# Moving two matrix products and one weight load at the start of a decoder block's turns

## The reference

```
x = x + attn(layernorm(x), ...)                       # 16 heads, stage A
x = x + gamma * xattn(layernorm(x), ctx, ctx)         # 8 heads of 64 rows, softmax over 512 columns
h1 = layernorm(x) @ w1q.T ; h3 = layernorm(x) @ w3q.T # 1365 hidden columns: "up"
x = x + (silu(h1) * h3) @ w2q.T                       # "down"
```

## Time and profile before

| | us |
|---|---|
| median of 3 runs | 1113.23 (1113.21 to 1115.01) |
| the profiled execution's own time | 1114.2 |
| its span, first to last instruction | 1112.1 |
| TensorE busy | 1104.1 |
| VectorE, ScalarE, GpSimd busy | 731.4, 550.5, 483.9 |
| DMA, mean rate | 110 GB/s |

### The profile page before, as it was taken

How to read it: one execution, slowest core, us unless ns; L and a number is a source line. 1 busy time by engine, 2 the same in 40 slices (tenths; PEclk the granted TensorE clock), 3 DMA queues, 4 the chain that set the end, 5 groups by cost and what they waited for, 6 DMA issues and landing times.

```text
span 1112.1 us, 15909 instructions
## 1 busy us (share of the span) xinstructions
PE 1104.1 (99%) x5840; PEld 938.7 (84%) x5840; DVE 731.4 (66%) x1347; ACT 550.5 (50%) x1149; POOL 483.9 (44%) x430
## 2 busy tenths in 40 slices
PE   9999999999999999999999999999999999999998
PEld 8888888878888888888888888888888888888886
DVE  7555547787777688866424334689967976887531
ACT  4556673324243376667515233167627763775130
POOL 1322327341424275665344040157728762875130
PEclk9999999999999999999999999999999999999999
DMA  7455553544533724212631112362113211310101
GB/s 246 164 189 189 185 176 129 171 126 159 173 111 93 230 96 142 86 39 86 252 114 38 38 59 65 140 205 63 53 52 101 77 49 58 113 49 1 38 1 38
DMA packets 54663, 122.20 MB, mean 110 GB/s; under 512 B 10057, under 2 KB 10057, under 8 KB 52538
## 3 DMA queue, kind: packets, MB, share of 16 engines
q1 hardware_dynamic: 54586, 121.18, 33.3%
HBM read 103.32 MB, written 17.84 MB: 109 GB/s over the span
## 4 chain that ended last, share of the span: by engine, by line
PE 94%; DVE 2%; DMA 1%; ACT 1%; issue 1%; POOL 0%; SPq 0%; POOLq 0%; DVEq 0%
PE bank L176 19%; PE bank L178 19%; PE bank L177 19%; PE bank L583 7%; PE bank L584 7%; PE bank L541 5%; PE bank L599 4%; PE bank L598 4%; PE bank L565 3%; PE bank L566 3%; PE bank L551 2%; PE bank L552 2%; DMA x1d<-x_scratch 1%; PE bank L608 0%; DVE x3l L860 0%
## 5 line engine op out<-in xcount | busy, mean ns | idle before, releaser
L583 PE MATMUL bank<-x3h,w 128*128 128x512 f32 (+2 forms) x368 | 143.5, 393 | 0.4 <-DVE x3l L860 0.3
L1471 ACT ACTIVATE yh<-bank 128x512 fp32r<-128x512 f32 x64 | 38.1, 600 | 209.9 <-PE bank L178 209.8
L584 PE MATMUL bank<-x3l,w 128*128 128x512 f32 (+2 forms) x368 | 140.6, 385 | 0.0
L940 POOL TENSOR_SCALAR pe_x<-pe_x,xri,gam 128x512 f32<-128x512 f32 x96 | 76.2, 795 | 78.5 <-DVE xri L779 76.1
L775 DVE TENSOR_REDUCE xmx<-bank 128x1 f32<-128x512 f32 x128 | 87.7, 687 | 32.9 <-PE bank L552 31.4
L2143 POOL TENSOR_TENSOR wal<-raw_a,wah 128x512 fp32r<-128x512 f32 x44 | 61.0, 1413 | 109.5 <-ACT wah L1513 109.5
L176 PE MATMUL bank<-wah,gh 128*128 128x512 f32 x256 | 102.6, 401 | 0.0
L2148 POOL TENSOR_TENSOR wbl<-raw_b,wbh 128x512 fp32r<-128x512 f32 x64 | 87.0, 1383 | 34.1 <-ACT wbh L1534 33.8
L176 PE MATMUL bank<-yh,rh 128*128 128x512 f32 x256 | 100.4, 392 | 0.8 <-DVE xacc L1979 0.8
L176 PE MATMUL bank<-wah,ph 128*128 128x512 f32 x256 | 100.1, 391 | 0.0
L177 PE MATMUL bank<-wal,gh 128*128 128x512 f32 x256 | 100.1, 391 | 0.0
(11 more groups left out here) (181 smaller groups left out, 3014.7 us busy)
## 6 DMA issues: line engine op xcount, KB each, us to landing
raw_a<-in_wk SPq DMA_DIRECT2D x8, 1024.0 KB, 5.2
raw_b<-in_wq SPq DMA_DIRECT2D x8, 1024.0 KB, 5.6
raw_a<-in_wo SPq DMA_DIRECT2D x8, 1024.0 KB, 5.1
raw_b<-in_wvt SPq DMA_DIRECT2D x8, 1024.0 KB, 5.0
ternary_scratch<-wraw SPq DMA_DIRECT2D x24, 341.2 KB, 3.0
x1d<-x_scratch SPq DMA_DIRECT2D x48, 128.0 KB, 3.1
kd<-in_ctx SPq DMA_DIRECT2D x48, 128.0 KB, 3.0
w<-ternary_scratch SPq DMA_DIRECT2D x2, 2730.0 KB, 11.1
```

The costliest lines, as they stand in the source:

```text
L583: pe.matmul(u_bank[w][0:m, cols], lhs, x3h[:, c, cols], start=c == 0, stop=False)
L584: mm = pe.matmul(u_bank[w][0:m, cols], lhs, x3l[:, c, cols], start=False, stop=c == CK - 1)
L940: pool.tensor_scalar(m.pe_x[:, q, :], m.pe_x[:, q, :], xri[:, q:q + 1], gam[:], ALU.mult, ALU.mult).then_inc(s["xpn"], 1)
```

## The change

`pieces` gets a table for the first five steps of every turn: products 0 and 1 together at step 1, product 2 at step 3, none at steps 0, 2 and 4. From step 5 on nothing differs (product 3 at step 5). Since ScalarE, VectorE and GpSimd read the same function, `th`, `uu`, `gf`, `gth` and `gtl` of these products move too. In `stage_b_sp`, W2 is issued behind the values of heads 2 and 3 and the rows and keys of head 3; before it was issued ahead of them. No instruction is added or taken away.

```
--- before.py
+++ after.py
@@ -396,8 +396,11 @@
 
         def pieces(n):
 
+
             if n < 0 or n >= S_TILES:
                 return range(0)
+            if n <= 4:
+                return (range(0), range(0, 2), range(0), range(2, 3), range(0))[n]
             return range(U_PIECES * n // S_TILES, U_PIECES * (n + 1) // S_TILES)
 
         def chunk_rows(i):
@@ -424,7 +427,7 @@
                 sp.wait_ge(s["vtl"], b * V_TILES + h // 2)
             sp.dma_start(m.vd[:], rows(ctx_cols, b)[h // 2]).then_inc(s["vd_in"], 16)
 
-        def sp_head(sp, m, b, h, values=True):
+        def sp_head(sp, m, b, h):
 
             slot, n = h % 2, b * XH + h
             if h >= 2 or b > 0:
@@ -434,7 +437,7 @@
                 part = slice(XD * half, XD * (half + 1))
                 sp.dma_start(m.x1d[part, slot, :], rows(x1_dram, b)[XD * h:XD * (h + 1), :]).then_inc(s[f"x1d_in{slot}"], 16)
                 sp.dma_start(m.kd[part, slot, :], rows(ctx, b)[XD * h:XD * (h + 1), :]).then_inc(s[f"kd_in{slot}"], 16)
-            if h % 2 == 0 and b > 0 and values:
+            if h % 2 == 0 and b > 0:
                 sp_vd(sp, m, b, h)
 
         def sp_values_early(sp, h):
@@ -511,10 +514,10 @@
             sp_x2_kept(sp)
             sp_x1_data(sp, p, 0)
             sp_x1_data(sp, p, 1)
-            sp_head(sp, main, 1, 2, values=False)
+            sp_head(sp, main, 1, 2)
+            sp_head(sp, main, 1, 3)
             sp_w2(sp)
-            sp_vd(sp, main, 1, 2)
-            for h in range(3, XH - 1):
+            for h in range(4, XH - 1):
                 sp_head(sp, main, 1, h)
             sp_x1_stat(sp, p, 0)
             sp_head(sp, main, 1, XH - 1)
```

## The result

| | before | after |
|---|---|---|
| median of the runs (8 each) | 1113.41 (1113.04 to 1115.01) | 1117.09 (1116.77 to 1120.67) |
| ratio after / before | | 1.0035, 95% interval 1.0025 to 1.0044 |
| span of the profiled execution | 1112.1 | 1115.2 |
| turn 1, 2, 3, from first score to first score | 108.82, 107.54, 107.90 | 109.22, 108.81, 109.12 |

The forecast was +2.4. The runs say +3.7, the profiled spans +3.1. (The forecast's 1115.6 stood on three runs of before, 1113.23; the eight give 1113.41, so 0.2 of the distance between 1117.09 and 1115.6 is that base.) Turns 1, 2 and 3 together are 2.9 longer; the other 0.2 is 0.12 in stage A and 0.09 in turn 4, where nothing was moved.

A forecast was written before the change was run, and what follows sets the result against it. TensorE was taken as the bound, busy 1104.1 of 1112.1 us. Turn 1's +0.3 and 2 x 1.05 for turns 2 and 3 gave +2.4, a span of 1114.5 and a median of 1115.6 us; range 1113.5 to 1117.4.

The forecast's parts named there:

- rival 3: GpSimd becomes the bound of the first steps, with `qst` late and a port block on the chain: +3.4, 1116.6, chance 0.16.
- W2's term: Turn 1: head 3's rows no longer queue behind W2, so VectorE's 2.23 wait goes: -1.0 (-0.78 to -1.28).
- Product 2's wait for bank 5: Turns 1 to 3: TensorE waits 1.08 for VectorE's `uu`, restarts with 0.11, saves the old 0.41: +0.78 a turn.
- The follower on VectorE: Tile 7's score waits for tile 5's exponential, 0.11 late plus 0.11 restart: +0.22 in each of turns 2 and 3.
- The follower on GpSimd: Tile 8's score waits for `qst` of head 2: +0.05 in each of turns 2 and 3, between nothing and 0.26.
- Rival 1: Product 2 doesn't wait for bank 5, so the kernel gets faster: 1110.8 to 1111.0, chance 0.07.
- rival 2: Only the bank's wait remains and the followers on VectorE and GpSimd vanish: +1.3, 1114.5, chance 0.22.
- Turn 1's products: Turn 1: the bank's wait, +0.78, and a VectorE follower made larger by three Newton instructions, 0.5 in place of 0.22.
- What was costed at nothing: Turn 1: head 4's rows behind W2, W2's later arrival and `sp_w2`'s wait for stage A's output, each without cost.
- part 1: W2 issued behind head 3's rows, turn 1 only: -1.0; a wait on rows or W2 anywhere would make it wrong.

The follow-up runs named there:

- `uu` first: The whole change, but VectorE does the `uu` of product 0 before the maximum of tile 2; 1114.87 us, ratio 1.0005 to the kernel before.
- `uu` first and `gf` late: The whole change, with product 0's `uu` before tile 2's maximum and product 1's `gf`, `gth`, `gtl` one step later; 1113.44 us, ratio 0.9994.
- `gf` late: The whole change, but `gf`, `gth` and `gtl` of product 1 one step later, as before; profiled span 1114.8 us, turn 2 109.03.
- all three: The kernel with `uu` first and `gf` late, plus GpSimd's four copies in steps 0 and 1; profiled span 1111.7 us, turn 2 108.04.
- copies early: The whole change, but GpSimd's four copies stand two each in steps 0 and 1; profiled span 1115.0 us, turn 2 108.68.

## Why the prediction was right in sign and short in size

The forecast, 1115.6 and slower, has the right mechanism. The measured +3.7 is 1.3 above its +2.4 and inside its range. It lies nearer to rival 3's number (+3.4) than to the forecast's. But of what the sum was short, only 0.4 is more time lost in turns 2 and 3, rival 3's reason; 0.8 is W2's term. Turn 2, 108.81, is just above the 108.5 to 108.7 that the forecast asked for.

**Product 2's wait for bank 5** (1.08 and 0.11, less the old 0.41): right. Measured 1.08 and 0.12 in turn 2; no wait at tile 2's score. The chain had `uu` start at 837.75 in a turn that began at 831.72; this one began 0.52 later, at 832.24, and `uu` started at 838.28, where the chain puts it to 0.01. The kernel with `uu` first shows the cause.

**The follower on VectorE** (0.22): right in size, 0.20, and partly by luck, since two errors cancel. The delay was 0.18 where the chain gave 0.11, and the restart that I added to it (0.11) is only 0.02 behind transposes. The delay was longer because I gave `x1d` the 0.54 from its start to the next start that the earlier trace rows show, where it began before GpSimd's `gtl`. (Undisturbed it is 0.44; there it had stood behind the end of a copy.) In the change `gtl` (842.62 to 843.91) begins first, and `x1d` (843.50) takes 0.61 to the next start. Rival 3 spoke of this block; it laid it on GpSimd's `pe_x` alone, which did get longer (0.93 in place of 0.77), but TensorE felt it through VectorE. The rule was the Trainium skill's (page "SBUF — State Buffer", section "SBUF: two separate sides"). The runs here agree with it, in both directions (`x1d` up to 1.30 in place of 0.53, `gtl` 1.53 in place of 1.30).

**The follower on GpSimd** (0.05, bounds 0 and 0.26): this step was mis-sized. `qst` was to end at 849.05 on before's clock, 849.57 with the 0.52 above, and it ended at 849.59. So the chain itself was right, and it gave the upper bound, 0.26; I talked it down because the `gtl` of 1.49 might lose its 0.19. It did, and `pe_x` took 0.16 back. Measured: 0.15 and a restart of 0.11, in turn 2 and again in turn 3. Together these turns came to +1.27 and +1.22, midway between the forecast's +1.05 and rival 3's +1.45. Rival 1, no wait for bank 5, and rival 2, no followers, are out.

**Turn 1's products** (0.78 + 0.5 = 1.28): 1.37 against the kernel with W2's move alone (109.22 - 107.85), of which 0.85 has gathered by tile 4's score and the rest is tile 7's. The second size (0.5) came out with only a part of its reason. The timeline of VectorE and GpSimd in turn 1, after:

```profile
732.82 0.69 DVE L778 TENSOR_REDUCE xmx<-bank 128x1 f32<-128x512 f32 x1 [0.84 <-PE bank L555]
...
734.43 0.78 POOL L943 TENSOR_SCALAR pe_x<-pe_x,xri,gam 128x512 f32<-128x512 f32 x1
...
734.69 0.80 DVE L767 TENSOR_SCALAR x1d<-x1d,stx 128x512 f32<-128x512 f32 x1
735.41 0.15 DVE L165 TENSOR_SCALAR rstd<-ntmp 128x4 int32<-128x4 int32 x1
735.59 0.69 DVE L778 TENSOR_REDUCE xmx<-bank 128x1 f32<-128x512 f32 x1
```

I had three Newton instructions on this chain. Two of them stand ahead of the maximum at 732.82, before which VectorE is idle for 0.84, so they delay nothing; the third (735.41) costs 0.18. As much again is `x1d`, which stands behind `pe_x`: 0.72 to the next start in place of 0.54.

**W2's move** (-1.0): this step failed, in two ways that the first profile could not tell. The mechanism is right for that one execution: the rows come in time, and turn 1 loses 0.97. But I took a landing time of one execution for a property of the kernel; in two others the old place costs 0.17 and 0.37. And I added this part to the others, where it overlaps: with the products moved TensorE and VectorE are late enough for the rows, and turn 1 is the same with either place of W2 (109.22; 109.10 and 109.12). So the change as a whole gets nothing for W2. Against the second profile of before, its turns are 1.20, 1.27 and 1.21 longer, in sum 3.7, which is what the runs show. With W2's term at 0.2 in place of 1.0, and 0.2 more in turns 2 and 3 each, the forecast's own sum would have been +3.6.

What was costed at nothing (head 4's rows behind W2, W2 itself, `sp_w2`'s own wait) showed no wait: head 4's rows are taken at 754.75 without one, though W2 is issued at 736.17, later than my 734. The forecast also said that a wait on rows anywhere would make part 1 wrong. There is one in turn 2 (0.46), but it is the products' doing and costs TensorE nothing, so it says nothing of W2.

**Is there a better version?** W2's move alone and the pair with `uu` first and `gf` late are both well below the change (ratios of 0.9995 and 0.9994 against 1.0035). Neither differs from the kernel before by more than the intervals can tell. Median spans are 0.85 and 0.35 below before's 1111.95, which is a sign and not shown.

## What to carry to other kernels

When two parts of a change act on the same engine within one stretch, price the second on the timeline that the first leaves: a wait that is worth 1.0 alone is worth nothing behind a new delay of the same length. Where a term rests on the landing of a DMA, one profile is one draw; look at a second before you credit it in full. And when a VectorE instruction moves against GpSimd's, ask which of the two starts first, since that decides where the time goes.

## What the runs showed of the hardware

`x1d` on VectorE (a scaling of 128x512 float32 from SBUF to SBUF) and GpSimd's `gtl` or `pe_x` do not run beside each other: the one that starts second stands until the first ends. Where `gtl` came first (after, `uu` first, `gf` late, all three), VectorE's next instruction starts 0.20 to 0.24 after `gtl`'s end. In turn 2 of the kernels with the products moved the price reaches TensorE nearly one for one at tile 7's score, 2 to 3 us later:

| kernel | `x1d` took | tile 7's score late by |
|---|---|---|
| `uu` first, `gf` late | 0.53 | 0.02 |
| after | 0.69 | 0.18 |
| copies early | 0.89 | 0.38 |
| `uu` first | 1.04 | 0.41, and 0.19 just before |
| `gf` late | 1.20 | 0.69 |
| all three | 1.30 | 0.80 |

The price is paid only where tile 7's score has nothing to spare. In the third profile of before, `x1d` began just behind a GpSimd copy and took 0.86; VectorE and GpSimd in turn 2:

```profile
840.99 0.61 POOL L950 COPY x2res<-x 128x512 f32<-128x512 f32 x1
...
841.02 0.86 DVE L764 TENSOR_SCALAR x1d<-x1d,stx 128x512 f32<-128x512 f32 x1
841.80 0.68 DVE L775 TENSOR_REDUCE xmx<-bank 128x1 f32<-128x512 f32 x1
```

Turn 2 is 107.54 there as in the other two profiles, where `x1d` took 0.61.

The trace does not call this a wait: it is in the instruction's duration, and no releaser is named. VectorE's instructions that read a PSUM bank (`uu`, `gf`, `pxl`, the maxima) show no such lengthening in these rows: 0.66 to 0.75 in all of them. The Trainium skill states the exclusive lock in the section named above. The delay of up to 0.77 here (1.30 less 0.53), larger than what the forecast gave to either follower, is what I had not expected.

The second thing is the spread of one DMA's landing: rows that stood behind W2 (2730 KB) in the same queue came between 20.6 and 21.5 after the start of the turn in three profiles of one kernel. W2 was issued 5.3 after the start in all three (728.18, 728.80, 728.59), so the spread lies between issue and landing. What makes it vary was not tried.
